# Reordering the stretch around the expert gather in a graph network kernel on one core

## What is computed

```
y = jnp.einsum('ecd,efd->ecf', buf, expert_w) + expert_b[:, None, :]
gathered = y[routes, jnp.minimum(pos, capacity - 1)]
out = jnp.where(keep[:, None], gathered, xf) * route_probs[:, None]
...
xn = _layernorm(x, axis=-1)
...
h = jnp.concatenate([x, agg], axis=-1)
h = jax.nn.relu(h @ W1 + b1)
return x + h @ W2 + b2
```

## Time and profile before

| | us |
|---|---|
| median of 3 runs (lowest, highest) | 880.34 (879.87, 881.35) |
| the profiled execution | 881.53 |
| its span, first to last instruction | 879.7 |
| PE busy | 791.9 (90%) |
| DVE busy | 617.6 (70%) |
| ACT busy | 382.4 (43%) |
| POOL busy | 115.8 (13%) |
| mean granted TensorE clock | 0.953 |

### The profile page before, as it was taken

How to read it: one execution, slowest core, us unless ns; L and a number is a source line. 1 busy time by engine, 2 the same in 40 slices (tenths; PEclk the granted TensorE clock), 3 DMA queues, 4 the chain that set the end, 5 groups by cost and what they waited for, 6 DMA issues and landing times. The chain is left out here.

```text
span 879.7 us, 11643 instructions
## 1 busy us (share of the span) xinstructions
PE 791.9 (90%) x4057; PEld 588.9 (67%) x4058; DVE 617.6 (70%) x1222; ACT 382.4 (43%) x583; POOL 115.8 (13%) x90
## 2 busy tenths in 40 slices
PE   5989999999999982698599999898797999999998
PEld 3777888888787861465287778655555566665776
DVE  7767776777658857598864323388787788988656
ACT  2342343332214413375221103766531788887453
POOL 3000000000000005010463001433600011100000
PEclk9999999999999995699589999999899899999999
DMA  5571321210302142999320302000000000010002
GB/s 179 154 244 64 100 69 56 71 58 2 126 0 84 61 171 95 254 376 313 96 96 1 96 0 91 6 0 2 1 1 2 2 1 1 1 54 1 1 1 96
DMA packets 48152, 66.63 MB, mean 76 GB/s; under 512 B 4268, under 2 KB 22460, under 8 KB 48095
## 3 DMA queue, kind: packets, MB, share of 16 engines
q1 hardware_dynamic: 43903, 56.22, 20.0%
q0 software_dynamic: 2384, 6.92, 2.4%
q10 hardware_dynamic: 1808, 2.75, 0.9%
HBM read 56.38 MB, written 9.50 MB: 75 GB/s over the span
## 5 line engine op out<-in xcount | busy, mean ns | idle before, releaser
L950 PE MATMUL bank<-xT,slot 128*128 128x512 f32 (+1 forms) x248 | 106.2, 428 | 2.3 <-DVE xT L1751 2.3
L952 PE MATMUL bank<-xT,slot 128*128 128x512 f32 (+1 forms) x248 | 98.3, 396 | 0.0
L951 PE MATMUL bank<-xT,slot 128*128 128x512 f32 (+1 forms) x248 | 98.2, 396 | 0.0
L1454 ACT ACTIVATE slot<-bank 128x512 fp32r<-128x512 f32 (+3 forms) x60 | 34.2, 586 | 136.8 <-PE bank L1214 56.3
L950 PE MATMUL bank<-slot 128*128 128x512 f32 (+1 forms) x212 | 83.6, 394 | 4.0 <-issue 1.8
L2270 DVE TENSOR_REDUCE key<-bank 128x2 f32<-128x1024 f32 x64 | 75.1, 1217 | 14.5 <-PE bank L1274 14.5
L952 PE MATMUL bank<-slot 128*128 128x512 f32 (+1 forms) x212 | 81.5, 384 | 0.0
L951 PE MATMUL bank<-slot 128*128 128x512 f32 (+1 forms) x212 | 81.5, 384 | 0.0
L950 PE MATMUL bank<-slot,xT 128*128 128x512 f32 (+1 forms) x192 | 79.0, 412 | 0.9 <-DVE xT L2122 0.9
L1679 ACT ACTIVATE arena<-bank 128x1024 f32<-128x1024 f32 x64 | 65.7, 1028 | 26.0 <-PE bank L1342 25.1
L952 PE MATMUL bank<-slot,xT 128*128 128x512 f32 (+1 forms) x192 | 76.5, 398 | 0.0
(11 more groups left out here) (335 smaller groups left out, 1701.8 us busy)
## 6 DMA issues: line engine op xcount, KB each, us to landing
arena<-in_ewT SPq DMA_DIRECT2D x16, 1024.0 KB, 12.4
arena<-in_edge_attr SPq DMA_DIRECT2D x16, 512.0 KB, 3.9
wraw<-in_qkvT SPq DMA_DIRECT2D x3, 1024.0 KB, 5.4
expert_rows<-rows SPq DMA_DIRECT2D x1, 2560.0 KB, 13.9
wraw<-in_L_ffn_expert_b POOLq DMA_DIRECT2D x16, 160.0 KB, 5.9
expert_results<-wraw ACTq DMA_DIRECT2D x16, 160.0 KB, 5.7
xn<-in_x SPq DMA_DIRECT2D x4, 512.0 KB, 6.5
wraw<-in_L_mix_w_qkv SPq DMA_DIRECT2D x2, 1024.0 KB, 7.9
```

The lines of the kernel that those rows point to most:

```text
L950: pe.matmul(out, L[1], R[0], start=start, stop=False, **kw)
L951: pe.matmul(out, L[0], R[0], start=False, stop=False, **kw)
L952: return pe.matmul(out, L[0], R[1], start=False, stop=stop, **kw)
L1454: act.activation(h, src, kw.pop("func", ACT.Copy), **kw).then_inc(hi_done, 1)
```

## The change

PE turns the aggregates right behind the last expert's rows, ahead of the product of expert 14, into banks 2 and 3, and multiplies them after the last expert. ACT in place of DVE takes them out of PSUM, ahead of the stores of experts 14 and 15; POOL in place of DVE writes the row of ones, and waits for the split of expert 14's weight. SP loads `w1e` after the same split. The tiles 0 to 3 are turned into banks 4 to 7. ACT takes the square roots of groups (0, 1) and (2, 3) ahead of all four evictions. DVE adds the gathered row of tile 4 and normalises tiles 2 and 3 ahead of the low parts of tiles 0 and 1, takes the moments of tile 4 between the low parts of tiles 1 and 2, and splits W2a after the low part of tile 3.

```diff
--- before.py
+++ after.py
@@ -155,13 +155,14 @@
     for e in range(EXPERTS + 1):
         if e < EXPERTS:
             add("eT", e, bank=4 + e % 2)
+        if e == EXPERTS - 1:
+            for g in range(2):
+                add("aggT", g, bank=2 + g)
         if e > 0:
             add("eY", e - 1, bank=6 + (e - 1) % 2)
+    for t in range(TH):
+        add("xT", 2, t, bank=4 + t)
     turn[0] = 0
-    add("aggT", 0)
-    add("aggT", 1)
-    for t in range(TH):
-        add("xT", 2, t)
     for hh in range(2):
         for th in range(2):
             for m in range(C):
@@ -830,7 +831,7 @@
             sp.wait_ge(res_ready, T)
             load_weight("W1a")
             load_weight("W2a")
-            finished(sp, "eY", EXPERTS - 1)
+            sp.wait_ge(ew_split, 2 * (EXPERTS - 1))
             sp.dma_start(w1e[0:EA], a["L1_gnn_W1"][D:D + EA]).then_inc(w1e_in, 16)
             sp.dma_start(w1e[EA:EA + 1], a["L1_gnn_b1"].rearrange("(a n) -> a n", a=1)).then_inc(w1e_in, 16)
             sp.wait_ge(res_ready, 2 * T)
@@ -880,6 +881,8 @@
                     emptied(pool, "eY", e - 4)
                 pool.dma_start(eb[e % 4], a["L0_ffn_expert_b"][e:e + 1].to_broadcast([CAPR, D])).then_inc(eb_in[e % 4], 16)

+            pool.wait_ge(ew_split, 2 * (EXPERTS - 1))
+            pool.memset(aggT[EA:EA + 1, :], 1.0).then_inc(blk_ready, 1)
             pool.wait_ge(route_ready, 3)
             for r in range(Y_RING):
                 pool.wait_ge(y_out[r], 16 * EXPERTS // Y_RING)
@@ -1192,6 +1195,12 @@
                     for k in range(C):
                         ins = pe.transpose(o[:, k * CAPR:(k + 1) * CAPR], xb[e][:, chunk(k)], ident[0:CAPR, 0:CAPR])
                     close(ins)
+                if e == EXPERTS - 1:
+                    for g in range(2):
+                        o = open_bank("aggT", g)
+                        for j in range(4):
+                            ins = pe.transpose(o[0:EA, chunk(j)], agg[:, 4 * g + j, :], ident)
+                        close(ins)
                 if e > 0:
                     m = e - 1
                     emptied(pe, "eT", m)
@@ -1202,12 +1211,6 @@
                         ins = mm3(o[0:CAPR, :], hl(xbT[m % 2], k), sl(m % 2, k), k == 0, k == C - 1)
                     close(ins)

-
-            for g in range(2):
-                o = open_bank("aggT", g)
-                for j in range(4):
-                    ins = pe.transpose(o[0:EA, chunk(j)], agg[:, 4 * g + j, :], ident)
-                close(ins)

             def from_aggregates(hh, th, m, start):
                 ch = hh * C + m
@@ -1596,14 +1599,18 @@
                 if e >= 2:
                     expert_high(e, 1)
                     send_y(act, e - 2)
+            act.wait_ge(ew_split, 2 * (EXPERTS - 1))
+            for g in range(2):
+                finished(act, "aggT", g)
+                act.activation(aggT[0:EA, g * HALF:(g + 1) * HALF], at("aggT", g)[0:EA, :], ACT.Copy).then_inc(evicted[bank_of[("aggT", g)]], 1)
             send_y(act, EXPERTS - 2)
             send_y(act, EXPERTS - 1)
             split_weight("W1a")
             split_weight("W2a")
             for g in range(2):
                 deviation(2, g)
-                for t in range(2 * g, 2 * g + 2):
-                    hi(("xT", 2, t))
+            for t in range(TH):
+                hi(("xT", 2, t))
             deviation(2, 2)

             for hh in range(2):
@@ -2160,11 +2167,6 @@
                         dve.wait_ge(y_out[y % Y_RING], 16 * (y // Y_RING))
                     dve.tensor_tensor(ey[y % Y_RING], at("eY", y)[0:CAPR, :], eb[y % 4], ALU.add).then_inc(evicted[bank_of[("eY", y)]], 1)
             split_weight("W1a")
-            split_weight("W2a")
-            for g in range(2):
-                finished(dve, "aggT", g)
-                dve.tensor_copy(aggT[0:EA, g * HALF:(g + 1) * HALF], at("aggT", g)[0:EA, :]).then_inc(evicted[bank_of[("aggT", g)]], 1)
-            dve.memset(aggT[EA:EA + 1, :], 1.0).then_inc(blk_ready, 1)
             dve.wait_ge(res_ready, T)
             dve.wait_ge(rows_sent, 16 * T)
             def routed(t):
@@ -2183,15 +2185,16 @@
                 for t in range(2 * g, 2 * g + 2):
                     routed_moments(t)
                 variance(2, g)
+            routed(TH)
+            normalise(2, 1, lambda t: xres[:, t, :])
             for t in range(2):
                 lo(("xT", 2, t))
-            normalise(2, 1, lambda t: xres[:, t, :])
-            routed(TH)
+            routed_moments(TH)
             for t in range(2, TH):
                 lo(("xT", 2, t))
-            for t in range(TH, T):
-                if t > TH:
-                    routed(t)
+            split_weight("W2a")
+            for t in range(TH + 1, T):
+                routed(t)
                 routed_moments(t)
             variance(2, 2)
             normalise(2, 2, lambda t: xres[:, t, :])
```

## The result

| | us |
|---|---|
| before, median of 8 runs (lowest, highest) | 880.24 (878.53, 881.66) |
| changed, median of 8 runs (lowest, highest) | 883.44 (881.71, 885.69) |
| changed, the profiled execution, its span | 885.69, 883.9 |

The ratio is 1.0037, with a 95% interval of 1.0022 to 1.0053: 3.2 us slower, where 1.6 us faster was forecast. The stretch around the gather did what was said of it. The loss lies 100 us behind it, in a place that the prediction never looked at.

A forecast was written before the change was run, and what follows sets the result against it. PE, busy 90% of the span, bounds the kernel; the question was when H(0,0) can start, held by the second gather's landing. Gains 0.5 + 1.13 = 1.63, say 1.65 us, take 880.34 to 878.7 us; range 877.2 to 880.2.

The forecast's parts named there:

- What follows is PE's and moves with it: After H(0,0) starts, 1.65 us earlier at 437.45, all later PE work was to shift by the same amount.
- The rest costs nothing: ACT's two evictions, the aggregates' products and W2a's later split were to add 0 us; tiles 4 to 7 had 3.7 us cover.
- only slower rival: Aggregates no longer fill PE before the tiles, so H(0,0) stays at clock 0.50; at worst 7.5 us lost, 886; chance 0.04.
- The clock: At H(0,0), beginning at 0.50 before and after; noise: the same start gives up to 1.0 us more or 0.6 less.
- The gathers: Second gather's landing, ahead of H(0,0): DVE's second row starts 0.5 us earlier; bounds 2.1 us earlier to 0.4 us later.
- The last sum: DVE's sum for the last expert: 8 transposes placed ahead of the last two products make it 0.4 us later.
- the 1.2 us by which POOL could begin earlier: Store of expert 15, with `w1e` loaded earlier, may land in 2.0 us, not 3.2; said to be worth nothing here.
- the lock: VectorE and GpSimd share a port pair exclusively, so POOL's descriptors wait for DVE's running split; without it, 1.6 us more gain.
- DVE's chain: From DVE's second gathered row to H(0,0): 13.73 - 1.89 + 0.94 - 0.2 = 12.6 us, 1.13 us saved.
- the first pause: DVE's 0.85 us wait before the first low part, blamed on PE's 7.17 us of aggregates' products delaying tile 0.
- taking these away alone gives nothing: Removing W2a's 2.25 us split, two copies and the 0.91 us row of ones from DVE before its second row gains nothing.
- point (c): POOL's first two gathers end some 0.9 us after a DVE split; with W2a's split moved, the second lands at 424.85.

## Why the prediction was wrong

- **The step that failed** is "What follows is PE's and moves with it", and "The rest costs nothing" with it. The part by part account took up every moved instruction, and not the moved line `turn[0] = 0`. That line renumbers the banks of all H, HW and csq jobs. I read the plan for the four tiles whose banks stand in the diff and left out those that follow from a counter. It cost 3.91 us of waiting and 1.54 of low clock.
- The forecast gave slower 0.04, and its only slower rival had the wrong mechanism. The clock did have a part, but behind a pause at csq, and not at H(0,0), where the low stretch grew shorter.
- **The gathers**: right in mechanism, and in size but for one term. The second row on DVE came 0.44 us earlier (0.5), the first gather ended 0.89 us after the split (0.9). The last sum came 0.14 us late, not 0.4. The store landed in 1.9 us, and the 1.2 us by which POOL could begin earlier were masked by the lock, as the run with `w1e` late shows.
- **DVE's chain**: the pauses went; from the second row to H(0,0) it took 438.20 - 425.84 = 12.36 us, where I had 12.6. H(0,0) won 1.81 us (1.65).
- **The clock**: H(0,0), up to the turning of tile 4, took 13.46 us before and 12.74 after. That step was called noise; it is 0.7 us, and it repeats: 12.55 to 13.02 us in the nine traces in which H(0,0) starts between 28.9 and 30.0, and 13.46 to 13.76 in the four in which it starts earlier or later. So 2.5 us had been won at csq.
- **What earns it**: the prediction charged the first pause to PE's aggregates, and said of W2a's split, the copies and the row of ones that "taking these away alone gives nothing", though its own point (c) has that split holding the second gather. The rows' order with W2a's split behind wins the whole 2.0 us; moving the aggregates adds nothing while W1a's split stands beside POOL.
- Rightly said to cost nothing: the row of ones on POOL, ACT's two evictions, W2a's split behind tile 3 (tile 5's row at 440.17, tiles 4 to 7 normalised by 447.9, wanted by PE at 450.94).

Open: against the kernel before on their chip, the first three versions without the pause (bank 2, the rows' order, the aggregates) gained 4.0, 3.5 and 2.3 us in the medians, and 2.5, 2.6 and 0.5 up to csq in their traces. The bank likewise costs 5.9 us in the trace of the kernel before and 5.5 in that of the changed one, but 3.3 and 6.3 in their medians. The traces are single executions, and the stretches at a granted clock of 0.50 behind 550 us differ between them: they add up to 14 to 24 us in the 13 traces, and in the two of the unaltered changed kernel to some 20 and 14 us, where 339.7 and 337.1 us passed from the first query product to the end. What makes up the rest was not settled.

## What to carry to other kernels

An edit that moves a counter, a turn or a seed moves everything that is numbered from it: list the resource of every later job before and after, not only those that the diff names, and ask for each new neighbour how late the old owner lets go. A read that stands late on its engine is free as long as nobody needs the buffer; such slack doesn't show in a profile's waits, since nothing waits for it. And when two edits remove the same wait, run each alone before crediting either.

## What was not expected of the hardware

- Where H(0,0) starts earlier, the granted clock need not rise earlier. Behind the last expert's transposes it rose at 36.4 us before (start 31.19), at 33.1 in the changed kernel (start 29.38), and at 33.2 with W1a's split between the stores (start 27.73): 1.8 us of earlier start brought the rise forward by 3.3, the next 1.6 by nothing. Up to csq, the first 1.81 us so counted 2.50, and the next 1.65 counted 0.86.
- The clock fell behind the pause of 3.8 us ahead of the query product; behind the one of 0.88, with csq in bank 5, it stayed.
- POOL's descriptor work is held until the end of DVE's running split, then takes 0.9 us. The same first gather took 2.71 us in the changed kernel, 2.38 with csq in bank 2, 1.29 with `w1e` late, and 1.02 with no split beside it. The memset on POOL did not slow DVE: its splits beside it took 1.21 us, as the others.
